# Score matmuls of a two-layer window attention that stream 64 key columns instead of 128

## The reference, cut to what matters

```python
x = x + L0(gn(x))   # window attention, 12 heads of 8 channels, 8x8 windows
x = x + L1(gn(x))   # window attention, 12 heads of 32 channels, windows shifted by 4, masks
x = x + L2(gn(x))   # depthwise 3x3 and pointwise convolution with quantised weights
x = x + L3(gn(x))   # spiking attention: q, k, v, k'v, q(k'v), projection
```

```python
attn = softmax(q @ k.T * scale + bias)      # 64 queries x 64 keys
out  = attn @ v
```

## Time and profile before

| | |
|---|---|
| device time, median of 3 runs | 680.67 us |
| the three runs | 677.33, 680.67, 831.42 us |
| span of the profiled execution, first to last instruction | 674.8 us |
| TensorE matmuls busy | 522.9 us (77%), 4459 instructions |
| VectorE busy | 479.1 us (71%) |
| ScalarE busy | 319.7 us (47%) |
| GpSimd busy | 304.6 us (45%) |
| mean granted clock of TensorE | 0.969 |

### The profile page before, as it was taken

One profiled execution on the slowest core, in us unless ns is written; L12 is line 12 of the kernel. 1 busy time (PEld: TensorE's weight loads), 2 busy tenths in 40 slices (PEclk: granted clock), 3 DMA queues, 4 the chain that ended last, 5 costly groups with the idle time before them and its releaser, 6 DMA issues.

```text
span 674.8 us, 13829 instructions
## 1 busy us (share of the span) xinstructions
PE 522.9 (77%) x4459; PEld 420.9 (62%) x4459; DVE 479.1 (71%) x1237; ACT 319.7 (47%) x746; POOL 304.6 (45%) x482
## 2 busy tenths in 40 slices
PE   0000087689999999986999999999999998867664
PEld 0000086678888888874788888888888772323432
DVE  0000357699999999985788888788888748966784
ACT  0000000447575756644466666666666553226673
POOL 9000001267676666673365545555555553340322
PEclk9999999999999999999899999999999999987786
DMA  1111300000000000000000000000000000000001
GB/s 58 47 54 47 89 9 0 1 1 2 1 0 0 0 0 0 0 1 1 1 1 3 1 0 0 0 0 0 0 0 0 0 1 1 0 1 0 24 23 47
DMA packets 9808, 7.04 MB, mean 10 GB/s; under 512 B 6371, under 2 KB 9443, under 8 KB 9667
## 3 DMA queue, kind: packets, MB, share of 16 engines
q1 hardware_dynamic: 3954, 5.01, 2.4%
q10 hardware_dynamic: 5826, 1.67, 1.2%
HBM read 5.11 MB, written 1.57 MB: 10 GB/s over the span
## 4 chain that ended last, share of the span: by engine, by line
PE 49%; DVE 19%; SPq 11%; issue 7%; POOL 7%; ACT 4%; DVEq 1%; DMA 1%; POOLq 0%; ACTq 0%
PE bank L749 16%; SPq L327 11%; PE bank L720 9%; PE bank L757 5%; PE bank L770 4%; PE bank L796 3%; DVE conv L1172 3%; DVE probs L913 3%; DVE xn L938 3%; PE bank L728 3%; DVE row_max L916 3%; PE bank L1253 3%; POOL probs L952 3%; PE bank L557 2%; POOL probs L947 2%
## 5 line engine op out<-in xcount | busy, mean ns | idle before, releaser
L749 PE MATMUL bank<-k,q 128*128 128x128 f32 x1536 | 216.1, 278 | 8.2 <-issue 4.5
L749 PEld LDWEIGHTS bank<-k,q 128*128 128x128 f32 x1536 | 199.3, 193 | 22.7 <-issue 7.2
L947 POOL TENSOR_TENSOR probs<-probs,row_max 128x384 f32<-128x384 f32 x128 | 106.0, 828 | 181.2 <-DVE row_max L916 180.5
L804 ACT ACTIVATE probs<-probs 128x384 f32<-128x384 f32 x128 | 67.1, 524 | 115.1 <-POOL probs L947 113.9
L952 POOL TENSOR_TENSOR probs<-probs,inv_sum 128x384 f32<-128x384 f32 x128 | 106.1, 829 | 3.7 <-DVE inv_sum L923 3.7
L913 DVE TENSOR_TENSOR probs<-bank,bias 128x384 f32<-128x384 f32 x128 | 71.1, 555 | 35.8 <-PE bank L749 33.4
L916 DVE TENSOR_REDUCE row_max<-probs 128x6 f32<-128x384 f32 x128 | 70.8, 553 | 4.4
L539 PE MATMUL bank<-pos,cst 64*128 64x16 f32 x32 | 7.0, 371 | 86.1 <-DMA pos<-in_L_conv_pos_emb 86.1
L921 DVE TENSOR_REDUCE row_sum<-probs 128x6 f32<-128x384 f32 x128 | 69.5, 543 | 2.2 <-ACT probs L804 2.1
L757 PE MATMUL bank<-cst,probs 128*128 128x128 f32 x384 | 64.3, 276 | 7.2 <-POOL probs L952 5.6
L809 ACT COPY probsT<-bank 128x384 f32<-128x384 f32 x128 | 59.9, 468 | 2.9 <-PE bank L757 1.7
(11 more groups left out here) (144 smaller groups left out, 854.8 us busy)
## 6 DMA issues: line engine op xcount, KB each, us to landing
rel_bc<-in_L_conv_rel_index SPq DMA_DIRECT2D x1, 1808.0 KB
x<-in_x SPq DMA_DIRECT2D x4, 384.0 KB, 32.6
out_dram<-y_out SPq DMA_DIRECT2D x8, 192.0 KB, 2.1
cst<-in_consts ACTq DMA_DIRECT2D x1, 613.5 KB
w<-in_L_conv_w_qkv ACTq DMA_DIRECT2D x1, 432.0 KB, 3.9
p<-in_L_conv_w_out ACTq DMA_DIRECT2D x4, 36.0 KB, 3.3
b_qk<-in_L_conv_qkv_b ACTq DMA_DIRECT2D x8, 0.1 KB, 5.4
pos<-in_L_conv_pos_emb SPq DMA_DIRECT2D x8, 2.0 KB
```

Of the source, the lines that this page charges most:

```text
L749: last = nc.tensor.matmul(ps_scores[w % 2][:, g * WT:(g + 2) * WT], q, k, start=True, stop=True)
L804: nc.scalar.activation(probs[w][:, :, :], probs[w][:, :, :], ACT.Exp).then_inc(L.s.exped, 1)
L947: nc.gpsimd.tensor_tensor(probs[w][:, :, :], probs[w][:, :, :], by_row(row_max[w]), ALU.subtract).then_inc(L.s.shifted, 1)
```

## The change

The key buffers lose their 64 spare columns, and a score matmul takes 64 keys and writes 64 columns of the bank. The number and order of the instructions on every engine stay as they are.

```diff
-        k0 = [sb(f"k0_{i}", [128, NU, T + WT]) for i in range(2)]
+        k0 = [sb(f"k0_{i}", [128, NU, T]) for i in range(2)]
...
-        k1 = [sb(f"k1_{i}", [128, NU, NP, T + WT]) for i in range(2)]
+        k1 = [sb(f"k1_{i}", [128, NU, NP, T]) for i in range(2)]
...
-            keys = slice(w * WT, (w + 2) * WT)
+            keys = slice(w * WT, (w + 1) * WT)
             for g in range(half * NP, (half + 1) * NP):
                 p, u = g // NU, g % NU
                 if L.wide:
                     q, k = q1[par][:, p, w, :, :], k1[par][:, u, p, keys]
                 else:
                     q, k = q0[par][:, w, p * NH:(p + 1) * NH, :], k0[par][:, u, keys]
-                last = nc.tensor.matmul(ps_scores[w % 2][:, g * WT:(g + 2) * WT], q, k, start=True, stop=True)
+                last = nc.tensor.matmul(ps_scores[w % 2][:, g * WT:(g + 1) * WT], q, k, start=True, stop=True)
```

## The result

| | before | after the change |
|---|---|---|
| device time, median | 679.0 us (4 executions) | 701.38 us (4 executions) |
| lowest and highest | 675.88, 831.42 | 685.83, 711.09 |
| span of the profiled execution | 674.8 us | 706.4 us (device time 708.49) |

The change made the kernel slower: the ratio of the comparison is 1.0201, with a 95% interval of 1.0105 to 1.0297, which leaves no doubt of the direction but not whether it is 2%. That ratio is formed from the two shortest of the four executions after the change (685.83 and 694.26), because the longer two were set aside as disturbed, although here the disturbance turns out to be the effect itself. The medians of all four stand at 1.033.

A forecast was written before the change was run, and what follows sets the result against it. TensorE alone was taken to bound L1, and a chain through VectorE, GpSimd and TensorE L0. From 680.7 us, -10.2 for group ends, +24 for low-clock samples and +3.5 for short spells gave 698 us, range 665 to 815.

The forecast's parts named there:

- The pace of a score matmul: Inside groups of score matmuls, the 128-column weight load sets the pace, 0.111 us, so 64 columns gain nothing there.
- The third rival: Score matmuls pace by columns, 0.053 us instead of 0.111: 636 us in all; chance 0.08.
- The ends of the groups: Last score matmul before transposes and before values ends 0.053 us sooner: L1 6.8 us, L0 3.4, sum -10.2 us.
- The clock at the start: L0's first 24 score matmuls stream half the time, so TensorE stays at 1.2 GHz beyond 124 us.
- The price of a low sample: An L0 sample at 1.2 GHz takes 19 us instead of 11, thus 8 us more.
- How many: Three samples' worth of L0 at 1.2 GHz, start and pause at 141 to 149 us together: +24 us.
- the same case: Clock lost for one to six samples of L0, 676 to 735 us; the likeliest case, chance 0.37.
- The steady part holds the clock at 2.4 GHz: Steady L0 and L1 keep 2.4 GHz, with streaming shares of 0.59 and 0.69 after the change.
- Lost in the pauses: The clock is lost in TensorE's pauses at 141 to 149 and 288 to 319 us.
- the second loss: Around 288 to 326 us, two short low-clock spells where one of 3.5 us exists now: +3.5 us.
- The clock stays: Rival: clock at 1.0 from some 130 us on, 670.5 us, bounds 667 to 677; chance 0.33.
- L0 stays low: Rival: L0 streams too little to leave 1.2 GHz, 735 to 799 us, 830 with part of L1; chance 0.22.

The follow-up runs named there:

- the second comparison: The changed kernel itself measured once more against the kernel before: seven executions from 685.75 to 723.31 us against 676.68, ratio 1.0134.

## Why the prediction was right, and where it was off

*The pace of a score matmul* was taken from the 96 and 16 column rows as the load's. Right: 0.62 and 0.71 us a group for 0.67 and 0.76 at 64 columns, about half of that gain at 96, and half of the pace (0.058 for 0.112) when the load was halved into two tiles. The third rival (pace by columns) fell.

*The ends of the groups.* L1 was to gain 6.8 us: 6.9 in the profile after the change, 7.7 with L0 left alone. For the transposes I had taken the whole 0.053 us against a bound of nothing; it was the whole. One sign did not come: the values were to start 0.16 us after the last score start instead of 0.21, and they start 0.205 after it as before; by the starts the 0.053 lies between the first two of a group. The size of the term was right, its place as forecast is not in the records. In L0 the term was over-sized: 0.21 us a sample forecast, 0.12 measured (11.08 to 10.96), 1.9 us in all for 3.4. Once a sample TensorE waits for the scaled probabilities behind the first group of scores:

```profile
226.69 0.81 PE L749 MATMUL bank<-k,q 128*128 128x64 f32 x6
227.77 0.55 PE L757 MATMUL bank<-cst,probs 128*128 128x128 f32 x3 [0.28 <-POOL probs L952]
```

From the scores to the transposes it is 1.08 us there, and was 183.81 - 182.82 = 0.99 before, so 0.09 us of the 0.21 is given back at this place.

*The clock at the start.* "The 24 first score matmuls will stream half of the time" and so not bring the clock up: right. They ran at 0.213 us and so did everything for 93 us. *The price of a low sample*: 8 us forecast, 7.9 measured (18.9 for 11.0). *How many*: three were assumed, the profiled execution had about five (93 us), and by the price of 7.9 us the eleven executions of this kernel (685.75 to 723.31) would have had some two to six; only two of them were profiled. This count is the term that was mis-sized. Of L0's +38.6 us, -1.9 are the groups and some +7 the loss at its end (below), so some +33 remain for the start, where the forecast had +24. That is also less than 93 x 0.42 = 39. In the kernel before TensorE had idle time in the first part of L0 (same columns as above), which is my estimate of where the difference went:

```profile
124.40:149.00 24.60, 19.49 (x190) 16.70 (x190) 21.58 (x60) 11.34 (x25) 12.74 (x17) 1.00 0.01 1
```

What sets the count stays open, the forecast's three were a guess, and the median moved with it: 701.4 in the first comparison, 686.3 in the second. So that 698 lies so near the first median is luck in the count, on top of the right mechanism; the second comparison would have met the low side of the same case (676 to 735).

*The steady part holds the clock at 2.4 GHz*: right, 102.6 us in the profile after the change and 140 us with the first sample wide. (The share of streaming in L1, put at 0.69, is about 0.72 by the prediction's own terms: 2.6 us less of 0.88 x 14.6. Nothing else was built on it.) *Lost in the pauses*: right, at both, shown by the kernel with the first sample wide. But the second loss was under-sized: I counted two spells of 3.5 us around 288 to 326, and it was one of 20.5 us (326.6 to 347.1) and one of 3.4. Its price follows from the kernel with the first sample wide: L0 there took 195.9 - 188.3 = 7.6 us more in spite of 1.9 us of gain, for 6.8 + 20.3 us at the low clock, thus 0.35 us for each of them: some 7 for the second where 3.5 had been put for both.

*The rivals.* The clock stays: refuted for this kernel, whose eleven executions all lie above its 677 and whose two profiles show the clock low; the loss disappeared when more was streamed at the start and in the pauses. L0 stays low: seen once, in the kernel with 64 columns in L0 alone (755.12), so its chance of 0.22 was not idle.

The Trainium skill's warning of idle gaps ("TensorE: Matmul & The Clock Gate", Part 1) would have let this pass: in the stretch from 124.4 to 217.4 us TensorE was busy 92.55 of 93 and the clock stayed low. The page's other sentence there, that activity releases the throttle, agrees with the streaming matmuls that brought the clock up before the first score.

## What to carry to other kernels

Work that nobody reads can be what brings TensorE up to 2.4 GHz at a start and behind a wait: before you take out padding columns, ask whether the load of the stationary operand sets the pace (then they cost only one column time per group) and how little will stream at the start and in the waits. Look at the spacing of a known instruction and not at the printed clock where no record exists. If the load is the pace, halve the load: two tiles side by side gave 3% here, and a handful of streaming matmuls placed in TensorE's own waits made up for the clock that narrow score matmuls had lost.

## What the runs showed that was not expected

The kernel before has rare executions far above the rest too: 831.42 us in the first comparison, and 923.62 in the second with a mean granted clock of 0.612, against 0.96 to 0.97 of its others. That mean says that the second of them had the low clock for some 715 of its 921.5 us. None was profiled, and what brings them about stays open.

That two tiles side by side keep the clock although each streams only 64 columns (up at 123.4 us) was against my expectation. The change of tile width, 0.11 and 0.15 us, was the only cost of the tiles that the timeline shows.
